# A two-layer DiT block on one core: the order table of all five engines within a sample set anew

## The reference

```python
mod = silu(c) @ w_mod + b_mod            # shift, scale, gate, twice
xn  = ln(x) * (1 + sc_msa) + sh_msa
q, k, v = split(xn @ w_qkv + b_qkv)      # 16 heads of 18
q, k = ln(q, g_q), ln(k, g_k)            # layer 0 only
attn = softmax(q k^T * 18 ** -0.5)
x = x + g_msa * ((attn @ v) @ w_proj + b_proj)
xn2 = ln(x) * (1 + sc_mlp) + sh_mlp
x = x + g_mlp * (gelu(xn2 @ w1 + b1) @ w2 + b2)
```

## Time and profile before

| | |
|---|---|
| time, median of 3 runs | 2543.11 us (2533.92 to 2545.91) |
| time of the profiled execution | 2542.38 us |
| its span | 2540.5 us |
| PE busy in the span | 2344.7 us (92%) |
| DVE, ACT, POOL busy | 1920.7, 1645.4, 720.7 us |

### The profile page before, as it was taken

The page is one execution under the profiler, slowest core; times in us unless marked ns, Lnnn a source line. Parts: engine busy times, 40 slices in busy tenths (PEclk is TensorE's granted clock), DMA queues, the critical chain, the costliest instruction groups (busy, mean ns, idle before and its releaser), DMA issues.

```text
span 2540.5 us, 75724 instructions
## 1 busy us (share of the span) xinstructions
PE 2344.7 (92%) x30337; PEld 1981.0 (78%) x30337; DVE 1920.7 (76%) x3456; ACT 1645.4 (65%) x3305; POOL 720.7 (28%) x938
## 2 busy tenths in 40 slices
PE   5558999999999999999899899999999999999998
PEld 3346887888887888887777788888888888888877
DVE  6457788778778788787676787788777787778764
ACT  3356777677677677676566666666666666666653
POOL 2011332233233233233231222233222322232222
PEclk8678999999999999999899999999999999999999
DMA  4786756765765765665755655555456555655531
GB/s 107 133 188 111 114 119 118 121 116 117 125 113 117 123 113 118 123 112 109 146 86 112 132 106 102 107 101 109 98 107 101 109 103 103 109 101 105 92 73 43
DMA packets 259284, 282.14 MB, mean 111 GB/s; under 512 B 25930, under 2 KB 243212, under 8 KB 258936
## 3 DMA queue, kind: packets, MB, share of 16 engines
q1 hardware_dynamic: 243888, 247.40, 53.1%
q10 hardware_dynamic: 15048, 29.89, 5.3%
HBM read 101.86 MB, written 26.73 MB: 51 GB/s over the span
## 4 chain that ended last, share of the span: by engine, by line
PE 58%; DMA 14%; DVE 12%; issue 6%; SPq 5%; ACT 3%; POOL 1%; DVEq 0%; ACTq 0%; POOLq 0%
PE psum L838 14%; PE psum L1082 13%; PE psum_max L838 8%; PE psum L961 6%; DMA attn_qk_squares<-qk_rstd 6%; DVE attn_maxima L1237 4%; PE psum_exp L838 4%; DMA x_between_layers<-mlp_x 4%; PE psum L828 3%; PE psum_max L950 3%; PE psum_exp L937 3%; DMA attn_k_stack<-attn_qk_hi 3%; DVE attn_qk_centred L1275 3%; SPq L1497 2%; PE psum L972 1%
## 5 line engine op out<-in xcount | busy, mean ns | idle before, releaser
L1237 DVE TENSOR_REDUCE attn_maxima<-psum_max 128x4 f32<-128x1024 f32 x512 | 621.5, 1214 | 212.9 <-PE psum_max L950 212.3
L1102 ACT ACTIVATE attn_probs<-psum_exp 128x1024 f32<-128x1024 f32 x512 | 523.7, 1023 | 157.8 <-PE psum_exp L937 146.8
L1410 POOL TENSOR_TENSOR mlp_x<-mlp_x,mlp_gated 128x288 f32<-128x288 f32 x128 | 127.7, 997 | 1093.4 <-DVE mlp_gated L1254 1093.4
L1082 PE MATMUL psum<-mlp_w_fc_hi,mlp_hidden_hi 64*128 64x288 f32 (+1 forms) x2250 | 347.0, 293 | 0.0
L1082 PE MATMUL psum<-mlp_w_fc_hi,mlp_hidden_lo 64*128 64x288 f32 (+1 forms) x2250 | 346.7, 292 | 0.0
L1082 PE MATMUL psum<-mlp_w_fc_lo,mlp_hidden_hi 64*128 64x288 f32 (+1 forms) x2250 | 344.8, 291 | 0.0
L961 PE MATMUL psum<-attn_probs,attn_v 128*32 128x256 f32 x4096 | 282.8, 394 | 1.6 <-DVE attn_neg_max_lo L1264 1.5
L838 PE MATMUL psum_max<-mlp_ln_split,mlp_w_fc_stacked 64*128 64x256 f32 (+1 forms) x3584 | 267.6, 284 | 11.2 <-DVE attn_maxima L1237 10.8
L950 PE MATMUL psum_max<-attn_k_stack,attn_q_stack 62*128 62x256 f32 x2048 | 219.2, 290 | 51.6 <-DMA attn_k_stack<-attn_qk_hi 35.3
L937 PE MATMUL psum_exp<-attn_q_stack,attn_k_stack 64*128 64x256 f32 x2048 | 246.0, 317 | 18.2 <-DMA attn_q_stack<-attn_neg_max_lo 5.7
L838 PEld LDWEIGHTS psum_max<-mlp_ln_split,mlp_w_fc_stacked 64*128 64x128 f32 (+1 forms) x3584 | 237.4, 189 | 29.9 <-DVE attn_maxima L1237 16.7
(11 more groups left out here) (184 smaller groups left out, 4485.9 us busy)
## 6 DMA issues: line engine op xcount, KB each, us to landing
attn_q_stack<-attn_qk_hi SPq DMA_DIRECT2D x256, 128.0 KB
attn_k_stack<-attn_qk_hi SPq DMA_DIRECT2D x256, 128.0 KB
attn_o_and_sums<-attn_o_transposed SPq DMA_DIRECT2D x256, 128.0 KB, 3.3
mlp_gate_and_gated_bias<-modulation ACTq DMA_DIRECT2D x64, 288.0 KB, 4.4
attn_qk_squares<-qk_rstd SPq DMA_DIRECT2D x32, 512.0 KB
attn_q_stack<-attn_qk_lo SPq DMA_DIRECT2D x128, 128.0 KB
attn_k_stack<-attn_qk_lo SPq DMA_DIRECT2D x128, 128.0 KB
attn_x<-in_x_dram SPq DMA_DIRECT2D x32, 288.0 KB, 3.0
```

The source lines that it names most:

```text
L1082: mm = q.matmul(to[t], (h_hi, h_hi, h_lo)[kind][r, c, t * P:t * P + P], (w2_hi, w2_lo, w2_hi)[kind][r, c, :], start=(i == 0 and not second ...
L1102: q.activation(probs[r][:], ps_exp[:], ACT.Exp, scale=SCORE_SCALE).then_inc(S["exps"], 1)
L1237: q.tensor_reduce(maxes[g % 2][:, p // QUARTER, :, p % QUARTER, :], ps_max[:].rearrange("p a (t n) -> p a t n", t=TT), AX.X, ALU.max).then ...
L1410: q.tensor_tensor(xt, xt, gated2[:], ALU.add).then_inc(S["added2"], 1)
```

## The change

Only the table of numbers and the choice of PSUM banks change; no instruction's code does. Besides the order, two things differ: in layer 0 the w_proj product is no longer cut into halves (`PROJ_FIRST` 27.5 to 26.5, `PROJ_SECOND` 28.0 to 27.0, with no slot of the scores between them now), and some steps use another bank (the turned MLP input of layer 0 goes to `psum_max` instead of `psum_exp`, the last chunk of the first linear layer to bank 7 instead of 6). Most single-sample exceptions are dropped. The lines that the prediction speaks of most:

```diff
-RSTD_OUT, RSTD_IN = -28.25, -23.25
-QK_Y = {4: -22.25, 0: -21.0, 1: -21.0, 2: -18.75, 3: -17.75}
-QK_LO = {4: -22.75, 0: -19.75, 1: -19.0, 2: (-17.0, -17.0, {ALL - 1: -19.0}), 3: -16.0}
+RSTD_OUT, RSTD_IN = -28.25, -25.25
+QK_Y = {4: -22.0, 0: -21.0, 1: -19.25, 2: -17.75, 3: -17.0}
+QK_LO = {4: -23.75, 0: -20.75, 1: -18.25, 2: -16.5, 3: -14.25}
...
-O_MOVE = [(10.25, 6.75, {B: 7.75, B + 1: 7.75}), (12.0, 10.75), (14.75, 12.75), (19.5, 18.5)]
+O_MOVE = [(10.25, 10.75), (12.0, 11.25), (18.25, 12.75), (19.5, 19.0)]
```

More of the change, by code:

```diff
@@ L91 @@
[L91 to L93 removed]
+QK_FIRST, QK_SECOND = [(-33.0, -26.0, {B - 1: -31.75}), (-32.75, -16.75)], [(-32.25, -25.0, {B - 1: -31.5}), (-32.25, -16.75, {2: -32.0, B - 1: -31.5})]
@@ new lines @@
+QK_OUT = {4: (-35.5, -27.5), 0: (-32.75, -24.25, {B + 2: -24.75}), 1: (-32.5, -24.25), 2: (-32.0, -16.5, {B + 1: -17.75}), 3: (-31.75, -16.5, {B + 1: -17.75})}
+QK_LOW = {4: -26.75, 0: -24.5, 1: -23.75, 2: (-15.5, -15.5, {B + 1: -16.5}), 3: (-15.5, -15.5, {ALL - 1: -14.0})}
+V_FIRST, V_SECOND, V_OUT = (-26.0, -17.75, {1: -31.0, B: -17.5}), (-25.5, -17.5, {1: -30.0, 2: -24.0, B + 1: -16.0}), [(-25.0, -17.5, {1: -29.5}), (-24.25, -16.75)]
+VAR_AT, RS_AT = (-28.75, -28.75, {B - 1: -29.0}), (-29.0, -29.0, {0: -31.5})
@@ new lines @@
+RSTD_OUT, RSTD_IN = -28.25, -25.25
+QK_Y = {4: -22.0, 0: -21.0, 1: -19.25, 2: -17.75, 3: -17.0}
+QK_HI = {4: -20.5, 0: -20.0, 1: (-18.0, -18.0, {0: -20.0, 1: -19.25}), 2: -17.5, 3: -16.5}
+QK_LO = {4: -23.75, 0: -20.75, 1: -18.25, 2: -16.5, 3: -14.25}
+TAILS_AT = [(-17.75, -24.5), (-16.0, -19.5)]
+STACKS_AT = {0: (-17.5, -17.5, {2: -16.5}), 1: (-15.75, -24.25, {ALL - 1: -21.5}), 2: (-15.75, -19.0, {2: -14.75}), 3: (-15.25, -16.0)}
+MAX_AT, MAX_OUT, MAX_TR, NEG_AT, NEG_PLACE = -11.5, -11, [(-4.25, -4.25), (3.75, 5.5, {ALL - 1: 3.0})], [(-4.5, -4.5), (4.25, 5.25)], [(-3.75, -6.0, {0: 0.25}), (5.5, 3.25, {B: 7.0})]
@@ new lines @@
+EXP_AT, EXP_OUT, PV_AT, PV_OUT = 0, 0.25, 5.75, 5.75
+O_MOVE = [(10.25, 10.75), (12.0, 11.25), (18.25, 12.75), (19.5, 19.0)]
+O_RECIP, O_NORM, O_HI, O_LO = (21.75, 20.5), (22.5, 22.5), (24.75, 24.75), (25.25, 26.75)
+XR_AT, GATE_AT, PROJ_FIRST, PROJ_SECOND = (23.75, 21.5, {B - 1: 23.25}), (24.0, 22.5), (26.5, 26.5), (27.0, 28.75)
+PROJ_OUT, PROJ_ADD = [(28.25, 28.5), (30.0, 29.5)], [(27.0, 31.5), (31.5, 32.75)]
+STATS2, RSTD2, NORM2, REST2 = [(30.0, 32.75), (33.0, 33.75, {B + 1: 36.25})], (34.75, 36.25), (36.75, 38.0), (37.75, 39.25)
@@ L94 @@
+TR2, Y2, SPLIT2, SPLIT2_LOW, GATE2_AT = (41.5, 41.5), (40.75, 40.75), (47.0, 44.25, {ALL - 1: 45.75, B: 45.0}), (49.25, 42.25, {ALL - 1: 43.75}), (50.0, 55.0)
+LAST_FC1_AT, FC1_AT, HIDDEN_AT, H_SPLIT = (49.75, 48.75, {B: 47.75}), 49.75, 49.75, [(49.75, 50.0), (49.75, 50.25), (50.0, 50.25), (50.25, 50.75), (50.5, 50.75)]
 FC2_PARTS = [(0, 0, 14), (0, 14, 27), (1, 0, 14), (1, 14, 27)]
-FC2_AT = [(49.75, 50.0), (51.5, 50.5), (55.0, 55.25), (56.5, 56.75)]
-FC2_OUT, FC2_ADD, STORE_AT = [(57.75, 58.25), (59.5, 61.0)], [(55.75, 58.5), (67.25, 69.0, {B + 2: 66.75})], (68.5, 66.5)
+FC2_AT = [(49.75, 50.0), (51.0, 50.5), (55.75, 55.5), (56.75, 57.25)]
@@ L97 @@
+FC2_OUT, FC2_ADD, STORE_AT = [(57.5, 58.25), (59.5, 61.0)], [(55.75, 58.5), (67.0, 69.0)], (68.5, 64.25)
 SLOTS = [FRONT + i / STEP for i in range(STEP * (SPAN * ALL + 72 - FRONT))]
@@ L112 @@
 TURN_BANKS, LN_REST_BANK, LN2_REST_BANK = ((4, 4), (7, 2)), (3, 7), (7, 7)
-FC1_FIRST, FC1_SECOND, LAST_FC1_BANK = (0, 1, 2, 3), ((5, 4, 0, 1), (5, 4, 0, 1)), (6, 6)
-QK_BANKS, LAST_CHUNK_BANK, VAR_BANK = [((4, 7), (4, 7)), ((5, 6), (6, 5))], (6, 7), 4
+FC1_FIRST, FC1_SECOND, LAST_FC1_BANK = (0, 1, 2, 3), ((5, 4, 0, 1), (6, 4, 0, 1)), (7, 6)
+QK_BANKS, LAST_CHUNK_BANK, VAR_BANK = [((4, 7), (7, 4)), ((5, 6), (6, 5))], (6, 7), 4
 V_BANKS, PROJ_BANKS, FC2_BANKS = ((4, 7), (7, 4)), ((7, 5), (7, 5)), ((5, 6), (5, 6))
-LN_BANK, LN2_BANK = (5, 5), (3, 0)
+LN_BANK, LN2_BANK = (5, 5), (1, 0)
 FC1_ORDER = [8, 0, 1, 2, 3, 4, 5, 6, 7]
```

16 lines of the change are left out of this document (2 added, 14 removed).

## The result

| | before | after |
|---|---|---|
| time, median of 4 runs | 2543.14 us (2533.92 to 2545.91) | 2496.34 us (2493.87 to 2499.15) |
| span of the profiled execution | 2540.5 us | 2496.4 us |

The ratio of the times, after to before, is 0.983 with a 95% interval from 0.9814 to 0.9845. So the kernel takes 43 us less by the ratio, 47 by the medians and 44 by the spans, where 29 had been forecast. The direction and the place were right, and the size was too small. Two further executions of the kernel before, at 2621 and 2713 us, showed a granted clock of 0.83 and 0.79 in place of 0.97 and are left out of all medians and ratios.

What follows compares the result with a forecast made beforehand. The prediction took PE to bound the kernel. It summed 26 steady layer 0 samples at −1.04 us (−27), six others (−4) and layer 1 (+2) to −29 us, so 2514 us; its own range was 2504 to 2524, for 8 in 10 2497 to 2536.

Steps and rivals of the forecast that it cites:

- What bounds the kernel: PE is the bound; to win are its 42 us idle in layer 0's steady stretch and its own work where that shrinks.
- The rival by which all waits go: Layer 0's steady 42 us of PE idle time and w_proj's saving all go: 2493 to 2504 us, chance 0.07.
- The stack transfers: Layer 0, SP: last stack transfer issued about 1.1 us sooner, so L950's wait falls from 0.79 to 0.2 us a sample.
- the largest rival: The stack is bound by its transfers, not its issue; L950's wait grows to about 1.4 us: 2536 to 2543 us, chance 0.15.
- The read of 1/rms: Layer 0, SP: ahead of L1504 it leaves 1.0 us sooner; DVE wins at most the 0.45 us it was idle.
- w_proj: Layer 0, PE: one piece instead of two halves saves 0.25 us a sample, bounds 0 and 0.4.
- DVE's stretch: Layer 0: pair L1288 and L1295 leaves it, 0.68 us; with the read up to 1.1, so L838's wait of 0.39 goes.
- The give-back of 0.2 us: Layer 0, PE: w_qkv's 28 products in one run want gated tiles and square sums: +0.2 us a sample, bounds 0 and 0.5.
- The other samples of layer 0: Six samples in the start and change of layers gain half the steady gain, 0.6 us each, together 4 us.
- Layer 1: POOL's new order delays L1246, mostly covered by DVE's idle time ahead of L1279: 0 to 7 us over 28 samples, taken as +2.
- the slower rival: Layer 1, POOL: L1439 held until L1356 ends, 1.8 us on 28 samples, +50 us, about 2562 us, chance 0.08.
- The other rival on DVE: Layer 1: L1370 loses 0.9 us beside later L1410 and L1412, samples 0.3 us longer: 2520 to 2528 us, chance 0.05.

Runs made afterwards that it cites:

- run 1: The changed kernel with the third move of o in layer 0 back among the 18 stack transfers: 2529.19 us, ratio to before 0.9953.
- run 2: The kernel before with only the third move of o in layer 0 put behind all stack transfers: 2526.04 us, ratio 0.9947.
- run 8: The kernel before with the third move of o behind the stack transfers and the read of 1/rms ahead of L1504: 2499.63 us, ratio 0.9845.
- run 5: The changed kernel with the read of 1/rms back behind L1504: 2524.48 us, ratio to before 0.9946.
- run 9: The kernel before with the move of o, the earlier read of 1/rms and layer 0's w_proj in one piece: 2500.12 us, ratio 0.9848.
- run 11: The kernel before with the move of o, earlier read of 1/rms, w_proj in one piece and pairs L1288 and L1295 later: 2494.87 us, ratio 0.9831.
- run 6: The changed kernel with layer 0's w_proj cut into halves again, L937 and L978 between them: 2512.30 us, ratio to before 0.9891.
- run 10: The kernel before with the move of o, earlier read of 1/rms and pairs L1288 and L1295 later on DVE: 2494.92 us, ratio 0.9829.
- run 7: The changed kernel with the pairs L1288 and L1295 back in DVE's stretch between the scores: 2499.04 us, ratio to before 0.984.
- run 4: The kernel before in layer 0, with the changed kernel's numbers for layer 1 and samples 32 and later: 2536.31 us, ratio 0.998.
- run 12: The changed kernel with POOL's order of layer 1 put back, L1439 behind L1410 and L1412 of the first tokens: 2495.83 us, ratio 0.9832.

## Why the prediction was right, and where it was too small

The forecast lacks 15 us against the spans. Of these 7.8 lie in 25 steady samples of layer 0 (1.36 us each against 1.04), and the rest outside them, mostly in the change of layers.

**What bounds the kernel: right.** PE's idle time in layer 0 was where the change worked. In the steady samples it fell from 1.54 us each (942 us with 903.52 busy) to 0.43 (908 with 897.22). The rival by which all waits go named the time, but not how: 0.43 us a sample are left, and 13.7 us came from the change of layers, where the rival looked at layer 0's steady stretch.

**The stack transfers: right, and the largest rival refuted.** Run 1 isolates the move of o: L950's wait is 28.0 us with it among the stack transfers and 3.5 without it, 0.15 a sample, where 0.2 was forecast. From the first of the 18 issues to the last SP takes 13.18 us in run 1 and 11.92 in the changed kernel (medians of 23 samples), about the 1.1 us of the prediction. The high DMA share of the earlier trace rows did not hold the landing.

**The read of 1/rms: the step that failed.** That it would leave 1.0 us sooner was right (1.2). The prediction took the 0.45 us that DVE was idle for it as the most that the read could give. That idle time was measured while PE also waited 0.79 us for the stack in each sample. Two ways lead from one sample to the next, one over the stack, the other over store, read and DVE, and they were nearly equally long. The 0.45 us was how much longer the one was at that place, not what it was worth. Run 2 shortens the first way alone, and DVE's wait for the read grows from 10.9 to 34.9 us. Run 8 shortens both. From run 2 to run 8 is 26 us, and from run 5 to the changed kernel 28 (0.6 and 1.1 us in each steady sample). The prediction summed three small separate gains, while the two large ones need each other: by the ratios the move of o is worth about 13 us alone (run 2) and 31 on top of the rest (run 1). The read alone in the kernel before was not run. That two such ways close from sample to sample is my reading of these waits; the times and the waits themselves are measured.

**w_proj: right in sign, wrong in why.** 0.25 us came from 2.30 us for the two halves, durations whose ends overlap with the next instruction. From start to start the halves take 1.07 and 1.03 us in run 8 (medians of 23 samples). The piece takes 2.05 in run 9, with L937 behind it as the halves have it, and 1.97 in the changed kernel with L978 behind it. So 0.05 to 0.13 is what the work shrinks by. Runs 9 and 11 show no gain from it. In the new order the piece is worth 0.45 us a sample (run 6), mostly as cover for L978. PE's busy time in the steady samples did fall by 0.25 us, from 36.13 to 35.88, but that agreement is luck. Runs 1 and 5 have the piece and are busy 36.14 and 36.10 us a sample; run 6 has the halves and is busy 35.79. What lowers it stays open.

**DVE's stretch: right that L838's wait goes, unclear by what.** The pairs remove it in the old order (run 10), and 0.25 of its 0.5 us reach the time. In the new order they may stand in either place at little cost (run 7). Whether the other moves on DVE opened that room was not isolated.

**The give-back of 0.2 us: about half, and for another tile.** The first products of w_qkv (L838) do wait now, 2.6 us in 24 samples, 0.1 each. They wait for ACT's copy of o (L1108), and not for the gated tiles and square sums that the prediction named.

**The other samples of layer 0: too small.** The forecast was 0.6 us each. The change of layers gave 13.7 us in seven. The chain of the kernel before shows its worst place, from 1217 to 1237 us:

```profile
1219.04 5.56 DMA x_between_layers<-mlp_x
1224.61 0.38 SPq L1504
1225.04 0.56 SPq L1471
1225.64 10.36 DMA attn_qk_squares<-qk_rstd
...
1236.42 1.22 DVE attn_maxima L1237
```

The same two transfers took 3.94 and 5.24 us in a steady sample. Here DVE was idle 6.10 us for the read, and PE 5.35 us at L978. With the move of o alone that wait of PE is still 5.28 us; with the read of 1/rms as well (run 8) it is gone, and one of 2.82 us at L937 stands near it. That sample takes 44.4 us before, 42.5 in run 2 and 38.4 in run 8. But the wait at L978 is gone in runs 4 and 5 too, where the read stands behind L1504. So the earlier read is enough and not needed, and what else removes this wait was not isolated. Half of a steady gain was no measure for a place with such a chain in it, and the profile before had it.

**Layer 1: the number right, its cause wrong.** +2 was forecast, +1.6 measured, 0.1 us a sample, although a growth of layer 1's samples was also named as a sign of being wrong. The forecast laid it to POOL's order. Run 12 shows that this order costs nothing, and the second wait for L1108 was not in the sum, so the agreement is luck. DVE's idle time ahead of L1279 went from 14.3 us to 2.4 over 22 samples (1500 to 2300 us) while L828's wait for it stayed at 0.24, so the slack was used up and just sufficed; with POOL's order put back it is 14.1 again. So the slower rival's price was nothing too. The other rival on DVE was half right. In the changed kernel:

```profile
L1370 DVE TENSOR_TENSOR mlp_hidden_lo<-mlp_hidden,mlp_hidden_hi 128x512 fp32r<-128x512 f32 x88 | 71.6, 814 | 3.0
...
L1327 DVE SCALAR_TENSOR_TENSOR attn_o_split<-attn_o_rest_hi,mask_of_rows_of_o,attn_o_and_sums 128x256 fp32r<-128x256 f32 x22 | 10.5, 478 | 0.0
L1370 DVE TENSOR_TENSOR mlp_hidden_lo<-mlp_hidden,mlp_hidden_hi 128x256 fp32r<-128x256 f32 x22 | 9.4, 425 | 0.7
```

Before, these took 693, 1026 and 888 ns. The mean of 814 hides what happens, which one sample shows (POOL's rows, then DVE's):

```profile
1911.01 0.80 POOL L1410 TENSOR_TENSOR mlp_x<-mlp_x,mlp_gated 128x288 f32<-128x288 f32 x1
1911.89 0.88 POOL L1412 TENSOR_TENSOR mlp_x<-mlp_x,mlp_gate_and_gated_bias 128x288 f32<-128x288 f32 x1
...
1911.14 0.96 DVE L1368 CAST mlp_hidden_hi<-mlp_hidden 128x512 fp32r<-128x512 f32 x1 [0.67 <-ACT mlp_hidden L1184]
1912.14 1.18 DVE L1370 TENSOR_TENSOR mlp_hidden_lo<-mlp_hidden,mlp_hidden_hi 128x512 fp32r<-128x512 f32 x1
...
1913.70 0.69 DVE L1370 TENSOR_TENSOR mlp_hidden_lo<-mlp_hidden,mlp_hidden_hi 128x512 fp32r<-128x512 f32 x1
```

One wide L1370 of four loses 0.5 us, and so does the cast L1368 ahead of it; the narrow one wins 0.46 and L1327 0.55. Together the three groups above and the wide cast L1368 are busy 141.4 us before and 142.5 after (1500 to 2300 us). The rival feared 0.9 us in one instruction; it got 0.5 in each of two and did not count what others win. No wait of PE followed from it.

## What to carry to other kernels

A wait at one place does not bound what the work behind it is worth when another wait stands beside it in the same cycle. Shorten one way in thought, let its gain arrive at the other, and only then read the slack. Here 0.45 us of DVE's idle time and the 0.79 that the other way gives make 1.24, an estimate; the read was worth 0.6 us a sample on top of the move of o alone and 1.1 in the new order.

On an engine that issues many transfers, look for an instruction that waits for a landing, and at what is queued behind it. Two such moves on SP brought 39 us of the 43 that the whole new table brings.

Read a saving on a pipelined engine from start to start, with the same instruction behind it, and test it in the order in which it will stand: the same w_proj was worth nothing in the old order and 0.45 us a sample in the new.

## What the runs showed of the hardware that was not expected

A two-input DVE instruction changes its length by over a factor of two with its neighbour on POOL. L1327 took 1026 ns beside L1410 and L1412 and 478 ns without them, and 1025 again when run 12 put them back. The Trainium skill, "SBUF — State Buffer", section "Who interferes with whom", describes such a shared port; these runs agree with it. In the sum over DVE the whole change shifted the cost to other instructions (L1370 and the cast L1368) and did not remove it. The two shifts are separate: when run 12 put L1327's neighbours back, L1370 stayed at 815 and 426 ns.

The same read of 1/rms took 5.24 us in a steady sample and 10.36 at the change of layers. What lengthened it there was not isolated.
